# A new slot order for the delta stage, and smaller moves in the sparse, local and global stages of an eight-stage model on one Trainium2 core

## The chip, the cores and the metric

The kernel runs on one core of one Trainium2 chip. The time is the device time of one execution in microseconds (us). A kernel's time is the median of its runs; of the kernel before there are three, 3733.58, 3734.76 and 3739.41. Engines are named as in the profile: PE (TensorE's matmuls), PEld (its weight loads), DVE (VectorE), ACT (ScalarE), POOL (GpSimd) and SP (SyncE, which issues DMAs).

## The reference

A stream of rows of 128 features runs through eight layers, each a residual on the layer norm of what came before (X holds them in 16 tiles of 128 rows):

```
x = x + delta(ln(x))      # gated delta rule, 8 value heads of 128, then a mixture of 8 experts, top 2
x = x + ternary(ln(x))    # one linear layer with weights in -1, 0, 1
x = x + chunks(ln(x))     # attention in chunks of 32, and over their means
x = x + ternary(ln(x))
x = x + sparse(ln(x))     # 16 heads of 8; only the 10 top queries of a head attend
x = x + local(ln(x))      # two layers: windowed attention of 8 heads, then a gated MLP
x = x + grouped(ln(x))    # 16 query heads, 4 key heads of 64, rotary, full softmax
x = x + local(ln(x))      # again, same weights
```

The delta rule, for each token and each head, is

```
S = S * exp(g)
S = S + k (v - k S) * beta
o = q S
```

It is computed in 16 tiles of 128 tokens. Within a tile the chain of tokens becomes a triangular system, whose inverse Y is built in five doubling levels (blocks of 2 x 64 rows): turn Y, multiply it from the right with the system, multiply from the left, put the new blocks into Y. Between tiles only the state S is handed on.

In the sparse stage a head's output is softmax(q k) v, divided by the row's sum and set to nought where the query is not valid; the local stage first shifts tokens by one for half of the features; the global one takes an exact row maximum from "rough" scores ahead and subtracts it in the real ones.

## The kernel before

Each stage is one function, called by `build_program` in the order delta, ternary, chunks, ternary, sparse, local, global, local. Within a stage each engine has its own list of steps, all in one order written by hand; semaphores tie them. There is no planner: an engine does its list in order, and a step that must wait holds up all behind it.

**Delta** (`delta_block`). `SLOTS` runs over the tiles and some more; in slot n an engine does steps of several tiles: projections and qk norms of tile n or n-1, first levels of the triangular system of n-1, last levels and reads of the state of n-2, the state and core of n-3, the experts of n-4. PSUM is eight banks, given to the products by the constants in lines 347 to 349; a step waits until the bank's last reader is through. The steps of which the prediction speaks:

- PE: `project_q/k/v/v2/z` (L387, L391 to 424), `grams`, `turn_Y(n, l)` (L486) turns Y of level l, `right_products` (L538), `left_products` (L587), `read_by_keys` and `read_by_queries` (L601, L612) multiply with the state, `solved`, `intra`, `state_sums` (L631 and on), `turn_core` (L656).
- DVE: `residuals` (L1080, L1081), `decayed_reads` (L1085), `update_Y` (L1071), `beta_decays` (L1028), `system` (L1036), `first_Y` (L1056 a copy, L1057 a predicated copy), `decayed_updates`, `core_sums` (L1112 to L1115), `norms` (L3348 on, a helper of 9 small operations), `add_state` (L1104), which ends in `state_ready`.
- POOL: `gate_matrices` (L963), `masked_decays` (L970), `weigh_z` (L974), `scale_state` (L982).

The state's loop goes: `read_by_keys(n)` -> `residuals` -> `solved` -> `updates` -> `decayed_updates` -> `state_sums` -> `add_state` -> `read_by_keys(n + 1)`.

**Sparse** (`sparse_attention`). ACT makes exponentials of the 80 x 2048 scores of each of two halves (g = 0, 1) (L2139); `scale_probs` multiplies them by the row's weight on DVE (L2204); `turn_probs` turns them on PE (L2099); DVE copies them out (L2209); `contexts` is 16 tiles of 128 x 80 (L2106); `rows_out`, the copy to `ow` (L2144) and the product of rows y (L2125) follow.

**Local** (`local_layers`). 32 items (two layers over 16 tiles), slot after slot; `keep_tokens` (L2553, L2554) copies the turned rows from PSUM to hT for the projection (L2331); ACT's slot begins with the squares of q and k (L2505) and ends with `keep_probs` (L2561).

**Global** (`grouped_attention`). 32 units of 8 spans j; each has scores of its queries over the keys, in rough form for the maximum (`part_max`, L3257) and then for real (L2984, L2986), contexts (L2997) and sums. `project(("q", u + 2))` (L2953) makes the queries of two units ahead, `turn_max` (L2975) the row maxima, `place_max` (L3273) puts these into `global_mrow`, `swap_halves` (ACT), `rotate` and `join_rotated` (L3252) make the rotary form. Keys are projected for only some units (`next_keys`).

## Time and profile before

| | us |
|---|---|
| median of three runs | 3734.76 |
| profiled execution | 3737.75 |
| its span in the trace | 3736.0 |
| PE, DVE, ACT, POOL busy over the span | 3254.7, 2669.1, 1946.8, 1687.1 |
| delta | 0 to 1071 |
| ternary, chunks, ternary | 1071 to 1237.4 |
| sparse | 1237.4 to 1369.6 |
| local | 1369.6 to 1796.5 |
| global | 1796.5 to 3303.3 |
| local | 3303.3 to 3736 |

The stage borders are read from the first instruction of each stage in the timeline. A row of a timeline reads: start, duration, engine, line, operation, what it writes and reads, shape; what stands in brackets at its end is how long the engine was idle before it, and which instruction's end released it. PEclk is the clock granted to TensorE as a share of its full rate. Times are us unless marked ns.

### The profile page before, as it was taken

Reading aid. Unit: us, or ns where it says so; the run is one execution under the profiler, and the core shown is the slowest. Engines: PE = TensorE matmul, PEld = TensorE weight load, DVE = VectorE, ACT = ScalarE, POOL = GpSimd, SP = SyncE. Lnnn points to the kernel's source line nnn. Section 1 sums busy time; section 2 is a strip of 40 time slices with the busy share of each in tenths; the row PEclk is TensorE's granted clock in tenths of the full one; section 3 lists DMA queues with packets and bytes.
Section 4 is the critical chain, followed back from the end, with each engine's and each line's share of the span. In section 5 each row is a group of like instructions: output and inputs, shape, how many; then the busy total and the mean of one; then the engine's idle time right before and its main releaser. Section 6 shows DMA issues by size and latency. Waiting matters only on the chain. (4 is left out here: it accounts for less than half of the span.)

```text
span 3736.0 us, 70352 instructions
## 1 busy us (share of the span) xinstructions
PE 3254.7 (87%) x27870; PEld 1992.5 (53%) x27870; DVE 2669.1 (71%) x4726; ACT 1946.8 (52%) x3456; POOL 1687.1 (45%) x1133
## 2 busy tenths in 40 slices
PE   5999999999747368998699999999999999969997
PEld 3667777777636256777333333333333333337776
DVE  4667667676655857777677777787778777667776
ACT  2445444444423219999344444444444444439997
POOL 0121212121114226665166666666666666756664
PEclk8999999999968669999799999999999999979999
DMA  2000000000010010000100000000000000010000
GB/s 95 2 1 2 2 2 1 2 2 2 2 54 2 6 55 1 2 2 2 30 1 1 1 1 1 1 1 1 1 1 1 1 1 1 1 46 2 2 2 13
DMA packets 22482, 31.76 MB, mean 8 GB/s; under 512 B 8610, under 2 KB 18252, under 8 KB 20940
## 3 DMA queue, kind: packets, MB, share of 16 engines
q1 hardware_dynamic: 22156, 27.26, 2.2%
q8 instruction: 223, 3.65, 0.4%
q14 instruction: 103, 0.84, 0.1%
HBM read 26.20 MB, written 1.05 MB: 7 GB/s over the span
## 5 line engine op out<-in xcount | busy, mean ns | idle before, releaser
L3190 POOL TENSOR_TENSOR global_acc_pool<-global_acc_pool,global_probs 128x1024 f32<-128x1024 f32 x320 | 796.6, 2489 | 246.3 <-ACT global_probs L3131 222.3
L3131 ACT ACTIVATE global_probs<-global_ps 128x1024 f32<-128x1024 f32 x512 | 519.9, 1024 | 626.6 <-PE global_ps L2986 611.2
L3257 DVE TENSOR_REDUCE global_part<-global_ps 128x2 f32<-128x1024 f32 x512 | 622.7, 1218 | 304.3 <-PE global_ps L2968 304.1
L2986 PE MATMUL global_ps<-global_q,global_k 64*128 64x512 f32 x2048 | 529.8, 595 | 0.0
L2997 PE MATMUL global_ps<-global_probs,global_v 128*64 128x512 f32 x2048 | 495.7, 605 | 0.0
L970 POOL TENSOR_TENSOR delta_etm<-delta_et,C_tile 128x1024 f32<-128x1024 f32 x16 | 40.2, 2514 | 755.6 <-ACT delta_et L853 755.6
L2968 PE MATMUL global_ps<-global_khh,global_qhh 64*128 64x512 f32 x1024 | 307.1, 597 | 59.0 <-DVE global_part L3257 52.0
L2984 PE MATMUL global_ps<-global_mrow,global_first 64*128 64x512 f32 x1024 | 321.1, 624 | 0.0
L2968 PEld LDWEIGHTS global_ps<-global_khh,global_qhh 64*128 64x128 f32 x1024 | 97.2, 187 | 375.9 <-DVE global_part L3257 300.5
L2997 PEld LDWEIGHTS global_ps<-global_probs,global_v 128*64 128x64 f32 x2048 | 124.2, 136 | 266.0 <-issue 178.2
L1071 DVE COPY_PREDICATED delta_Yd<-delta_tri,delta_ps 64x512 f32<-64x512 uint32 x160 | 116.6, 729 | 191.3 <-PE delta_ps L587 188.8
L2986 PEld LDWEIGHTS global_ps<-global_q,global_k 64*128 64x128 f32 x2048 | 196.5, 188 | 91.6 <-issue 62.8
L387 PE MATMUL delta_ps<-delta_wconv,delta_x1T 128*128 128x512 f32 x512 | 236.4, 606 | 2.7 <-PEq L50 1.5
L2496 ACT ACTIVATE local_sm<-local_ps,local_nb,local_rn 128x128 f32<-128x128 f32 x512 | 226.3, 463 | 15.8 <-DVE local_nb L2682 14.5
L862 ACT ACTIVATE delta_NTp<-delta_ps 64x512 f32<-64x512 f32 x176 | 104.1, 591 | 242.6 <-PE delta_ps L538 219.6
L3190 DVE TENSOR_TENSOR global_acc<-global_acc,global_probs 128x1024 f32<-128x1024 f32 x128 | 215.2, 1681 | 7.9 <-ACT global_probs L3131 7.9
L3112 ACT ACTIVATE global_swapped<-global_ps 32x512 f32<-32x512 f32 x192 | 112.8, 588 | 144.2 <-PE global_ps L2953 142.3
L857 ACT ACTIVATE delta_T<-delta_ps 64x512 f32<-64x512 f32 x176 | 104.0, 591 | 132.0 <-PE delta_ps L486 128.7
L2984 PEld LDWEIGHTS global_ps<-global_mrow,global_first 64*128 64x128 f32 x1024 | 98.1, 188 | 111.7 <-issue 100.1
L2593 POOL TENSOR_TENSOR local_sm<-local_sm,local_rden 128x1024 f32<-128x1024 f32 x64 | 121.4, 1897 | 65.3 <-DVE local_rden L2725 65.1
L2638 POOL TENSOR_TENSOR local_qkr<-local_qkr,local_rn 128x512 f32<-128x512 f32 x64 | 70.5, 1102 | 174.6 <-DVE local_rn L3356 174.6
L387 PEld LDWEIGHTS delta_ps<-delta_wconv,delta_x1T 128*128 128x128 f32 x512 | 94.9, 193 | 101.3 <-issue 97.0
(584 smaller groups left out, 7090.5 us busy)
## 6 DMA issues: line engine op xcount, KB each, us to landing
delta_cw<-in_conv_taps SPq DMA_DIRECT2D x4, 1024.0 KB, 10.6
local_tab<-in_rot_tables SPq DMA_DIRECT2D x2, 2048.0 KB, 12.4
local_tab<-in_rot_tables SPq DMA_DIRECT2D x2, 1536.0 KB, 7.7
localw_wqkv<-in_L_ffn_wqkv SPq DMA_DIRECT2D x2, 768.0 KB
delta_wqkvz<-in_L_attn_a_W_qkvz SPq DMA_DIRECT2D x1, 1024.0 KB, 5.6
local_tab<-in_rot_tables SPq DMA_DIRECT2D x2, 512.0 KB, 4.2
global_cos<-in_rope_cos SPq DMA_DIRECT2D x8, 128.0 KB, 3.3
global_sin<-in_rope_sin SPq DMA_DIRECT2D x8, 128.0 KB, 3.3
```

The costliest lines, as they stand in the source:

```text
L387: mm = pe.matmul(banks(bank), x1T[:, P * n + j:P * n + j + P], wconv[:, j, column:column + 512], start=(j == 0), stop=(j == TAPS - 1))
L1071: ins = dve.copy_predicated(Yd[own, n % 2], over_middle(tri[own, l + 1], HV), blocks(DELTA_BANK + s)[own])
L2496: ins = act.activation(sm[:, k % 2, g, :], ps[:, SC + part, P * i:P * i + P], ACT.Exp, bias=nb[:, k % 2, g:g + 1], scale=rn[:, k % RN, hea ...
L2593: pool.tensor_tensor(sm[:, k % 2], sm[:, k % 2], over_inner(rden[:, k % 2, :], P), ALU.mult)\
L2968: mm = pe.matmul(ps[:, first_bank + s, :], qhh[own, u % 2, P * qt:P * qt + P], khh[own, group_of(u) % 2, BLK * c:BLK * c + BLK], start=Tru ...
L2984: pe.matmul(ps[:, 2 * (at % 2) + s, :], first[own, :], mrow[own, u % 2, :], start=True, stop=False)
L2986: mm = pe.matmul(ps[:, 2 * (at % 2) + s, :], k2[own, group_of(u) % 2, P * k:P * k + P], q[own, u % 3, :], start=False, stop=True)
L2997: mm = pe.matmul(ps[own, 4, :], v[:, k, HD * g:HD * g + HD], probs[:, at % RING, BLK * s:BLK * s + BLK], start=(k == 0), stop=(k == TILES ...
L3112: ins = act.activation(swapped[32 * a:32 * a + 32, :], ps[32 * b:32 * b + 32, proj_bank(n), :], ACT.Copy, scale=1.0 if a % 2 else -1.0)
L3131: act.activation(probs[:, at % RING, :], ps[:, 2 * (at % 2):2 * (at % 2) + 2, :].rearrange("p b n -> p (b n)"), ACT.Exp).then_inc(S["probs ...
L3190: ins = eng.tensor_tensor(sums[:, u % 2, :], sums[:, u % 2, :], probs[:, at % RING, :], ALU.add)
L3257: dve.tensor_reduce(part[:, u % 2, r % SLOTS, :], ps[:, rough_banks(r), :], X_AXIS, ALU.max)\
```

## The change

In the delta stage all engines get a new order within the slot, and the PSUM banks are given out anew; every wait that follows from these two is adapted. `SLOTS` has one more turn. Slot n now does q, k, v, v2 and decays of tile n, which were split between n and n + 1 before, and state_sums of n - 2, which was n - 3. In the sparse stage the weights of rows are applied in the copy to `ow`, and the contexts of both halves become one chain of 32 matmuls of 160 columns where there were two of 32 (16 tiles in two passes) with 80. In the local stage `keep_tokens` goes from ACT to DVE and is one slot earlier. In the global stage the projection of q stands behind the first contexts of span 0, not ahead of it, its rotation is one span later, and `place_max` stands ahead of the join of the keys.

The delta stage: constants, GpSimd's list and VectorE's list.

```diff
-QK_BANK, V_BANK, Z_BANK, QKT_BANK, DECAY_BANK, GRAM_BANK, KS_BANK, QS_BANK, W_BANK = 2, 2, 0, 2, 2, 2, 0, 4, 0
-INTRA_BANK, STATE_BANK, CORET_BANK, GATEUP_BANK, OUT_BANK, X2T_BANK, ROUTER_BANK, HIDT_BANK, DOWN_BANK = 0, 4, 6, 2, 3, 4, 4, 3, 5
-T_BANK, NTP_BANK, DELTA_BANK = 6, 4, 0
+QK_BANK, V_BANK, Z_BANK, QKT_BANK, DECAY_BANK, GRAM_BANK, KS_BANK, QS_BANK, W_BANK = 2, 2, 6, 0, 6, 2, 2, 0, 6
+INTRA_BANK, STATE_BANK, CORET_BANK, GATEUP_BANK, OUT_BANK, X2T_BANK, ROUTER_BANK, HIDT_BANK, DOWN_BANK = 0, 4, 4, 4, 3, 1, 2, 2, 5
+T_BANK, NTP_BANK, DELTA_BANK = 0, 4, 6
...
-SLOTS = range(0, TILES + 4)
+SLOTS = range(0, TILES + 5)
...
         for n in SLOTS:
-            if valid(n - 4):
-                weigh_z(n - 4)
+            if valid(n - 2):
+                scale_state(n - 2)
+            if valid(n):
+                gate_matrices(n)
             if valid(n - 1):
                 masked_decays(n - 1)
-            if valid(n):
-                gate_matrices(n)
-            if valid(n - 3):
-                scale_state(n - 3)
+            if valid(n - 2):
+                weigh_z(n - 2)
...
         for n in SLOTS:
-            if valid(n - 3):
-                decayed_updates(n - 3)
-                core_sums(n - 3)
             if 0 <= n - 1 < TILES + LAG_ROW:
                 norms(n - 1)
             if valid(n - 3):
                 add_state(n - 3)
-                normalize_core(n - 3)
+            if valid(n - 4):
+                normalize_rows_2(n - 4)
             if valid(n - 1):
                 scale_qk(n - 1)
-            if valid(n - 4):
-                normalize_rows_2(n - 4)
-            if valid(n - 2):
+            if valid(n - 3):
+                normalize_core(n - 3)
+            if valid(n - 2):
+                decayed_reads(n - 2)
                 residuals(n - 2)
-                decayed_reads(n - 2)
-            if valid(n - 1):
-                beta_decays(n - 1)
-            if valid(n - 2):
                 update_Y(n - 2, 2, 0)
                 update_Y(n - 2, 2, 1)
             if valid(n - 1):
-                probs(n - 1)
-            if valid(n - 4):
-                logits(n - 4)
-            if valid(n - 1):
+                beta_decays(n - 1)
                 system(n - 1)
                 first_Y(n - 1, 0)
                 first_Y(n - 1, 1)
-            if valid(n - 4):
-                choose(n - 4)
+                probs(n - 1)
             if valid(n - 2):
                 update_Y(n - 2, 3, 0)
                 update_Y(n - 2, 3, 1)
-            if valid(n - 3):
-                add_rows(n - 3)
             if valid(n - 4):
+                logits(n - 4)
+                choose(n - 4)
                 routes(n - 4)
+                hidden(n - 4)
             if valid(n - 1):
                 update_Y(n - 1, 0, 0)
                 update_Y(n - 1, 0, 1)
-            if valid(n - 4):
-                hidden(n - 4)
             if valid(n - 2):
                 update_Y(n - 2, 4, 0)
                 update_Y(n - 2, 4, 1)
+            if valid(n - 3):
+                add_rows(n - 3)
             if valid(n - 1):
                 update_Y(n - 1, 1, 0)
                 update_Y(n - 1, 1, 1)
             if valid(n - 2):
                 update_Y(n - 2, 5, 0)
+                updates(n - 2)
+                decayed_updates(n - 2)
+            if valid(n - 4):
+                add_experts(n - 4)
             if valid(n):
                 qk_sums(n)
             if valid(n - 2):
-                updates(n - 2)
-            if valid(n - 4):
-                add_experts(n - 4)
+                core_sums(n - 2)
```

PE's slot n after, tile in brackets, and ACT's changes:

```
PE:  read_by_queries(n-2) read_by_keys(n-2) turn_qk(n-1) left(n-2,2) turn_core(n-3) turn_x2(n-4)
     grams(n-1) turn_Y(n-2,3) project_z(n-1) right(n-2,3) turn_Y(n-1,0) left(n-2,3) right(n-1,0)
     router(n-4) turn_Y(n-2,4) gate_and_up(n-4) left(n-1,0) out_rows(n-3) right(n-2,4)
     turn_Y(n-1,1) left(n-2,4) right(n-1,1) turn_hidden(n-4) turn_Y(n-2,5) left(n-1,1)
     right(n-2,5) project_q(n) left(n-2,5) turn_Y(n-1,2) solved(n-2) down(n-4) project_k(n)
     intra(n-2) right(n-1,2) project_v(n) decays(n) state_sums(n-2) project_v2(n)
ACT: keep_hidT(n-5) first; place_blocks(n-3) early, not place_blocks(n-2) last; silu_qk(n-1) between
     keep_T and keep_NTp of (n-2,2); keep_qkT before keep_coreT; router_exp and silu_gate together
```

The sparse stage:

```diff
         def turn_probs(g):
-            pe.wait_ge(A["probs_ready"], g + 1)
+            pe.wait_ge(A["probs_exp"], g + 1)
...
-        def contexts(g):
-            pe.wait_ge(A["probsT_ready"], g + 1)
+        def contexts():
+            pe.wait_ge(A["probsT_ready"], 2)
             for t in range(TILES):
-                mm = pe.matmul(ps[:, 4 * g + 3, 0:HALF], v_all[:, t, :], probsT[:, g, t, :],
+                mm = pe.matmul(ps[:, 7, 0:H * TOP], v_all[:, t, :], probsT[:, :, t, :],
                                start=(t == 0), stop=(t == TILES - 1))
             mm.then_inc(A["o_ps"], 1)
 
         def rows_out(g):
-            pe.wait_ge(A["oT_ready"], g + 1)
+            pe.wait_ge(A["oT_ready"], 1)
             pe.matmul(ps[0:HALF, 5 + g, 0:DIM], oT[:, 8 * g:8 * g + 8, :].rearrange("p h r -> p (h r)"),
                       wT[:, 3, :], start=True, stop=True).then_inc(A["ow_ps"], 1)
 
         turn_probs(0)
-        contexts(0)
         turn_probs(1)
-        contexts(1)
+        contexts()
         rows_out(0)
         rows_out(1)
...
             act.wait_ge(A["ow_ps"], g + 1)
-            act.activation(ow[:, g, :], ps[0:HALF, 5 + g, 0:DIM], ACT.Copy).then_inc(A["ow_ready"], 1)
+            act.wait_ge(A["weights_ready"], g + 1)
+            act.activation(ow[:, g, :], ps[0:HALF, 5 + g, 0:DIM], ACT.Copy, scale=srow[:, g:g + 1]).then_inc(A["ow_ready"], 1)
...
-        def scale_probs(g):
+        def row_weights(g):
             dve.wait_ge(A["probs_exp"], g + 1)
             own = srow[:, g:g + 1]
             link(dve.reciprocal(own, own))
-            link(dve.tensor_tensor(own, own, valid[:], ALU.mult))
-            dve.tensor_scalar(probs[:, g, :], probs[:, g, :], own, None, ALU.mult).then_inc(A["probs_ready"], 1)
+            dve.tensor_tensor(own, own, valid[:], ALU.mult).then_inc(A["weights_ready"], 1)
...
-        def own_heads(g):
-            dve.wait_ge(A["o_ps"], g + 1)
-            own = slice(8 * g, 8 * g + 8)
-            dve.tensor_tensor(oT[:, own, :], heads(ps[:, 4 * g + 3, 0:HALF], 8), over_inner(hm[:, own], TOP), ALU.mult)\
-                .then_inc(A["oT_ready"], 1)
-
-        scale_probs(0)
-        scale_probs(1)
         keep_probs(0)
         keep_probs(1)
-        own_heads(0)
-        own_heads(1)
+        row_weights(0)
+        row_weights(1)
+        dve.wait_ge(A["o_ps"], 1)
+        dve.tensor_tensor(oT[:], heads(ps[:, 7, 0:H * TOP], H), over_inner(hm, TOP), ALU.mult)\
+            .then_inc(A["oT_ready"], 1)
```

The local stage, then the global stage (PE, ACT, DVE):

```diff
-SLOTS = range(-3, ITEMS + 7)
+SLOTS = range(-4, ITEMS + 7)
...
-        def keep_tokens(m):
-            t = m % TILES
-            act.wait_ge(S["xT_ps"], m + 1)
-            act.activation(hT[UP, tokens(t)], ps[UP, TURN, 0:P], ACT.Copy)
-            act.activation(hT[DOWN, P * t + 1:P * t + P + 1], ps[DOWN, TURN, 0:P], ACT.Copy)\
-                .then_inc(S["hT_ready"], 1)
-
...
                 gelu(n - 4)
-            if valid(n + 3):
-                keep_tokens(n + 3)
             if valid(n - 2):
                 keep_probs(n - 2)
...
+        def keep_tokens(m):
+            t = m % TILES
+            dve.wait_ge(S["xT_ps"], m + 1)
+            dve.tensor_copy(hT[UP, tokens(t)], ps[UP, TURN, 0:P])
+            dve.tensor_copy(hT[DOWN, P * t + 1:P * t + P + 1], ps[DOWN, TURN, 0:P])\
+                .then_inc(S["hT_ready"], 1)
...
                 row_stats(n - 2)
+            if valid(n + 4):
+                keep_tokens(n + 4)
...
         for u in range(UNITS):
             for j in range(SPANS):
-                if j == 0 and u + 2 < UNITS:
-                    pe.wait_ge(S["mrow_ready"], u + 1)
-                    project(pe, ("q", u + 2))
...
                 if j == 2 and u:
                     out_sums(pe, u - 1)
+                if j == 0 and u + 2 < UNITS:
+                    project(pe, ("q", u + 2))
                 if at + 1 + AHEAD < UNITS * SLOTS:
                     rough_scores(pe, at + 1 + AHEAD)
...
-                if j == 0 and u + 2 < UNITS:
+                if j == 1 and u + 2 < UNITS:
                     swap_halves(("q", u + 2))
...
-                if j == 0 and u + 2 < UNITS:
+                if j == 1 and u + 2 < UNITS:
                     rotate(("q", u + 2))
-                if j == 1 and u + 2 < UNITS:
+                if j == 2 and u + 2 < UNITS:
                     join_rotated(("q", u + 2))
...
                 if j == 6 and next_keys(u):
                     rotate(next_keys(u))
+                if j == 7 and u + 1 < UNITS:
+                    place_max(u + 1)
                 if j == 7 and next_keys(u):
                     join_rotated(next_keys(u))
-                if j == 7 and u + 1 < UNITS:
-                    place_max(u + 1)
```

## Rows read from the trace of the kernel before

**Rows 1.** The windows view by stages: us, busy (x) per engine, PEclk, DMA, GB/s

```profile
0.00:1071.00 1071.00, 942.14 (x11302) 711.65 (x11302) 686.77 (x1233) 447.11 (x621) 152.82 (x72) 0.96 0.03 10
...
1369.60:1796.50 426.90, 365.19 (x3836) 286.49 (x3836) 322.65 (x957) 370.56 (x955) 246.86 (x260) 0.96 0.04 14
```

**Rows 2.** Timeline of VectorE: state additions, the first and the last of 14

```profile
161.23 1.22 DVE L1104 TENSOR_TENSOR delta_state<-delta_ps,delta_state 128x1024 f32<-128x1024 f32 x1 [0.26 <-issue]
...
937.94 1.22 DVE L1104 TENSOR_TENSOR delta_state<-delta_ps,delta_state 128x1024 f32<-128x1024 f32 x1
```

**Rows 3.** Timeline of TensorE at the hole, and two windows behind it

```profile
460.39 1.33 PE L538 MATMUL delta_ps<-delta_T,delta_NT 64*64 64x64 f32 x32 [2.04 <-DVE delta_state L1104]
...
461.60:465.00 3.40, 3.40 (x12) 2.72 (x10) 2.44 (x4) 3.19 (x4) 0.00 (x0) 0.56 0.00 0
...
465.00:470.00 5.00, 5.00 (x60) 4.48 (x59) 4.72 (x4) 2.40 (x4) 0.00 (x0) 1.00 0.00 2
```

**Rows 4.** Timeline of VectorE and GpSimd ahead of a state addition

```profile
331.32 2.30 DVE L1113 TENSOR_TENSOR delta_sq<-delta_core 128x1024 f32<-128x1024 f32 x1
...
335.50 2.21 DVE L3348 TENSOR_SCALAR delta_rn<-delta_ss 128x17 int32<-128x17 int32 x1
...
332.50 2.88 POOL L982 TENSOR_TENSOR delta_state<-delta_state,delta_eg 128x1024 f32<-128x1024 f32 x1
```

**Rows 5.** One line each: min/median/max ns; and GpSimd's timeline at 945

```profile
L1028 DVE TENSOR_TENSOR delta_etb<-delta_et,delta_nbeta x16: 1214/1215/1787, 57.7 to 946.4; 128x1024 f32<-128x1024 f32 x16
...
945.12 1.99 POOL L982 TENSOR_TENSOR delta_state<-delta_state,delta_eg 128x1024 f32<-128x1024 f32 x1 [9.09 <-PE delta_ps L612]
...
L1056 DVE COPY delta_Yd<-C_tile x32: 418/422/426, 68.1 to 953.9; 64x512 f32<-64x512 f32 x32
...
L1057 DVE COPY_PREDICATED delta_Yd<-delta_tri,delta_NT x32: 726/740/753, 68.6 to 954.3; 64x512 f32<-64x512 uint32 x32
```

**Rows 6.** Timelines of the first local stage: three slot starts, TensorE's and VectorE's start

```profile
1427.62 1.05 ACT L2505 ACTIVATE local_qksq<-local_ps 128x1024 f32<-128x1024 f32 x1
...
1723.54 1.05 ACT L2505 ACTIVATE local_qksq<-local_ps 128x1024 f32<-128x1024 f32 x1
...
1734.92 1.05 ACT L2505 ACTIVATE local_qksq<-local_ps 128x1024 f32<-128x1024 f32 x1
...
1380.08 3.24 PE L2331 MATMUL local_ps<-localw_wqkv,local_hT 128*128 128x512 f32 x4
...
1382.16 0.22 DVE L2787 CAST local_identr<-C_tile 128x128 fp32r<-128x128 f32 x1
```

**Rows 7.** Timeline of the sparse stage, ScalarE then TensorE; one window at the query products

```profile
1329.23 0.19 ACT L2139 ACTIVATION_READ_ACCUMULATOR sparse_probs<-sparse_ps,sparse_mrow 80x1 f32 x1
...
1340.74 2.34 PE L2099 MATMUL sparse_ps<-C_tile,sparse_probs 80*128 80x80 f32 x16
...
1344.79 7.11 PE L2106 MATMUL sparse_ps<-sparse_probsT,sparse_v_all 128*128 128x80 f32 x32 [1.71 <-DVE sparse_probsT L2209]
...
1353.31 14.03 PE L2125 MATMUL sparse_ps<-sparse_ow,sparse_selT 80*128 80x128 f32 x64 [0.36 <-ACT sparse_ow L2144]
...
1309.70:1316.70 7.00, 7.00 (x34) 6.83 (x34) 4.64 (x22) 0.00 (x0) 0.00 (x0) 0.65 0.01 2
```

**Rows 8.** Timeline of the global stage: join, hole, turn_max starts, and one window

```profile
1990.07 1.71 DVE L3252 TENSOR_TENSOR global_k<-global_rot 128x512 f32<-128x512 f32 x1
...
1992.43 1.12 PE L2953 MATMUL global_ps<-global_xnT,globalw_wq 128*128 128x512 f32 x2 [1.70 <-DVE global_mrow L3273]
...
1995.00:1998.00 3.00, 3.00 (x12) 1.25 (x12) 0.13 (x1) 2.94 (x5) 0.26 (x1) 0.63 0.00 0
...
1985.11 0.33 PE L2975 MATMUL global_ps<-C_tile,global_nmx 128*128 128x128 f32 x1
...
2176.71 0.33 PE L2975 MATMUL global_ps<-C_tile,global_nmx 128*128 128x128 f32 x1
...
2220.03 0.33 PE L2975 MATMUL global_ps<-C_tile,global_nmx 128*128 128x128 f32 x1
```

More of the change, by code:

```diff
@@ L608, in read_by_queries @@
                     pe.wait_ge(S["qkT_ready"], n + 1)
-                    pe.wait_ge(PAIRED["NTp_ready"][n % 2], step(n, 2, 1))
+                    if n >= 1:
+                        pe.wait_ge(S["core_sums"], n)
+                    else:
+                        pe.wait_ge(PAIRED["T_ready"][n % 2], step(n, 2, 1))
                     for h in range(HK):
@@ L744, in _ @@
                 for n in SLOTS:
-                    if valid(n - 1):
-                        project_v(n - 1)
-                    if valid(n - 3):
-                        state_sums(n - 3)
-                    if valid(n - 1):
-                        project_v2(n - 1)
-                    if valid(n - 2):
-                        right_products(n - 2, 2)
-                        read_by_keys(n - 2)
-                    if valid(n - 3):
-                        turn_core(n - 3)
                     if valid(n - 2):
                         read_by_queries(n - 2)
+                        read_by_keys(n - 2)
                     if valid(n - 1):
@@ L761, in _ @@
                         left_products(n - 2, 2)
+                    if valid(n - 3):
+                        turn_core(n - 3)
                     if valid(n - 4):
@@ L818, in _ @@
                     if valid(n - 2):
-                        intra(n - 2)
+                        solved(n - 2)
+                    if valid(n - 4):
+                        down(n - 4)
+                    if valid(n):
+                        project_k(n)
+                    if valid(n - 2):
+                        intra(n - 2)
+                    if valid(n - 1):
+                        right_products(n - 1, 2)
+                    if valid(n):
+                        project_v(n)
+                        decays(n)
+                    if valid(n - 2):
+                        state_sums(n - 2)
+                    if valid(n):
+                        project_v2(n)
             @block.scalar
```

226 lines of the change are left out of this document (131 added, 95 removed).

## The prediction

> **What bounds the kernel now.** I read the stage windows first (one core, stages one after the other), then each stage's timeline. The delta stage is TensorE's: 942 of 1071 us busy at a granted clock of 0.96 [rows 1]. Its steady slot lasts (937.94 - 161.23)/13 = 59.75 us [rows 2], and the only large hole of TensorE in it is one of 2.0 us per slot behind VectorE's state addition (L1104) [rows 3]. The local stages are ScalarE's: 370.6 of 426.9 us [rows 1], 11.84 us per slot. The global stage is TensorE's, with a hole of 1.70 us in some of its units [rows 8]. The sparse stage is one chain over PE, DVE and ACT, in which every operation counts [rows 7].
>
> The sum is made against the profiled run, 3737.75 us, which is 3.0 above the median of 3734.76.
>
> **Delta: the hole that goes.** Ahead of the state addition VectorE does, before, decayed updates, core sums and norms. Two of these meet GpSimd: L1113 takes 2.30 us [rows 4], where L1028, of the same operands, takes 1.21 [rows 5], and L3348, only 17 columns wide, takes 2.21; exactly there GpSimd runs gate matrices, state scaling (L982, itself 2.88 where it takes 1.99 elsewhere) and z weights back to back [rows 4, 5]. After, core sums stand at the slot's end, GpSimd has nothing in flight there, and the chain is 9.1 - 1.1 - 2.0 = about 6 us. The state comes 11.5 us after project_k, by my count of L1112 to L1104 at free durations; PE gets to read_by_queries 13.5 us after it, since intra, right(2), v, decays, state_sums and v2 now stand between. So the hole closes: -2.0 us per slot. Behind it TensorE's granted clock was 0.56 for 3.4 us [rows 3], mostly the lower of its two levels (1.2 and 2.4 GHz), which costs 3.4 x 0.44 = 1.5 us; it does so in about every second slot (the starts of L1104 are 59.0 and 60.7 apart by turns), so another -0.8. That leaves 56.95.
>
> **Delta: the wait that comes.** GpSimd now starts at read_by_keys(n-2) (K) with scale_state, gate_matrices, masked_decays, weigh_z; K is also what VectorE's residuals wait for, and behind these stand, on VectorE, update_Y(2), beta_decays, system and both first_Y(n-1). TensorE waits for first_Y in turn_Y(n-1,0), having after K only left(2), turn_core, turn_x2, grams, turn_Y(3), z and right(3) to do, about 9.1 us. On VectorE the chain is 2 x 1.22 + 2 x 0.74 + 1.22 + 1.29 + 2 x (0.42 + 0.74) = 8.75, with links about 9.5 us: hole 0.4. But L1081, L1028 and the copy L1056 have only SBUF operands and meet GpSimd. The row for that is the last of L1028's 16, at 946.4, the only one that started behind a running L982 (945.12 to 947.11): 1.79 us, not 1.21 [rows 5]. L1056 and L1057 never met GpSimd before (418 to 426 and 726 to 753 ns) [rows 5], so their price has to be bounded: nothing, or all of the masked_decays (2.4 us) and gate (1.9 us) that lie there. With GpSimd and VectorE alternating I get L1081 +0.5, L1028 +0.8 and the copy +1.7, first_Y at K + 12.4, so a hole of about 3.35 us. That is 60.3 us per slot; behind so long a hole the clock probably falls again as behind the old one, I take two slots of three at 1.5: +1.0, 61.3. The other holes that I find (at turn_Y(n,1), left(n-1,4), right(n,1)) are 0.2 to 0.3 and replace ones of the same size. Moving projections one slot earlier and the new banks only change which wait is met first; I count them at nothing, the cover being the PE work ahead of each. 61.3 - 59.75 = +1.55, over 14 full slots: **+22 us**. Ends: 57.6 (copy not held up, hole 0.4 and 0.25 of others: -30) to 62.1 (low clock each time and the others: +33).
>
> The Trainium skill (SBUF — State Buffer, section "SBUF: two separate sides") has the same pair of ports behind both engines: an exclusive lock, kept for a whole instruction by whichever starts first. By that rule a VectorE operation that has started first makes GpSimd wait instead, and the chain would slip less than I count; the trace agrees as far as it goes, L982 having started first and L1028 having waited.
>
> **Local, twice.** ACT loses the two hT copies. The 25 slots from 1427.62 to 1723.54 take 11.84 each; the one behind them, 1723.54 to 1734.92, has no such copy and takes 11.38 [rows 6]. The difference, 0.46, less 0.02 for a row maximum that then comes last, times 25 is -10.9 per stage (bounds 0.35 to 0.57 per slot); VectorE, busy 323 of 427 us [rows 1], hides the copies at the slot's end. The start pays: hT of the first tile now comes only when DVE is through with the mask and identity casts, 1382.16 + 0.22, and two rounds of turn and copy behind that, so that project_qk (L2331) starts at about 1384.5, not at 1380.08 [rows 6]: +4.4. Net -6.5 per stage, **-13** for both (-20 to -9).
>
> **Sparse.** Scaling leaves the chain; the weights go into the ow copy on ACT, which has slack since they are ready long before the contexts. turn_probs(1) can start when the second exponential ends, 1329.42; from its start to the contexts it was 1344.79 - 1340.74 = 4.05, so the joined contexts start at 1333.5 [rows 7]. The query products (L2079), 32 matmuls of 160 columns, took 7.0 us at a granted clock of 0.65 [rows 7]; at the lower level that is 9.1, at the upper 4.5. They end at 1342.6, where the old ones ended at 1351.9; the rows y (L2125) keep their distance of 1.4: start 1344.1 instead of 1353.31. **-9** (matmuls of 7 us: -11; of 4.5: -14; one us of order lost: -8).
>
> **Global.** In units that join keys, DVE's join (1.71) stands ahead of place_max, and TensorE waits 1.70 us in project(q) for it, then runs at a granted clock of 0.63 [rows 8]. A plain unit lasts 43.32, as from 2176.71 to 2220.03 (turn_max, L2975, one of 14 such). The stretch 1985.11 to 2176.71 is four units: 191.6 [rows 8]. The two others of this kind took 190.1 and 191.8; sum 573.5. After: place_max stands ahead of the join and the projection behind the first contexts, so the row maxima come 1.71 us earlier, which is all of the hole of 1.70: they are ready as TensorE gets to the scores. Four units are 4 x 43.32, three key projections of 1.25 and 0.3 for each late join: 178.3. That is 573.5 - 535 = **-39**, and -1 for units that are not in a stretch. If only the hole goes and the clock does not rise, 12 x 1.7 = 20; if the join then holds up part_max by its 1.71 and nothing hides it, -20 as well. Bounds -24 to -55 (holes of 0.4 in plain units gone too). Moving q's rotation from j 0 to 1 costs at most the 0.3 per unit that lies under TensorE's work.
>
> **Sum.** 3737.75 + 22 - 13 - 9 - 40 = 3697.75; less 3.0 for the median: **3695**.
>
> **The rivals.** (A) The copy wins: first_Y is not held up, the slot is 57.6, delta -30. For it: the same copies never took over 0.43 us. Against it: they never met GpSimd. 3695 - 52 = 3643. Chance 0.27. (B) The change does not do in the global stage what it says: the maxima are late all the same, since rough scores and part_max of the span before set them, and the hole moves to the scores; -10 and not -40: 3725. For it: 1.71 and 1.70 leave nothing to spare. Chance 0.12. (C) Slower: the new hole of 3.4 us in the delta stage is followed by the low clock not for 3.4 us of work but for all up to the next full slot. It decides at a slot of 64.8 us, that is 5.05 x 14 = +70, eating the -62 of the others and 7.5 beyond; this takes 6.5 us more of TensorE's work at half speed than I count. Against it: behind the hole at 460.39 the clock was 1.00 again from 465 on [rows 3]. At 65 us it gives 3695 - 22 + 74 = 3747. Chance 0.05. The forecast itself: 0.56.
>
> **How the numbers follow.** 3695 is the forecast's. Its own range is 3672 (sparse -14, local -20, global -51) to 3717 (delta +33; sparse, local and global half way to their small ends, +1, +2 and +8). The 8-in-10 range goes from below A (global gain 10 more than counted) to B: 3632 to 3724. About 0.2%, 7.5 us, is what a measurement of this kernel can tell from no change; 3727 is its lower edge. Faster: forecast 0.56, A 0.27, 0.05 of B's: 0.88. Same: the rest of B's, 0.07. Slower: 0.05.
>
> **What would show it.** In the profile after: no hole in front of L601 and L1113 at 1.22 (right), a wait of TensorE in turn_Y (L486) for first_Y (L1057) of 3 us and a copy L1056 near 2 us (right; at 0.42 it is A); slots of L1104 at 61.3; 11.40 between L2505 starts; L2975 starts 43 to 45 apart all along; L2125 9 us earlier after its stage begins. Wrong would be a gap in front of a step that I took for covered: state_sums or decays waiting for UD, or qk's silu one slot late.

## The result and the profile after

The changed kernel takes 3646.05 us in the median of four runs (3643.54 to 3650.88), beside 3736.91 for the kernel before (four runs). The ratio is 0.9759, with a 95% interval of 0.9744 to 0.9773: 91 us or 2.4% faster. The forecast was 3695, its range 3632 to 3724. The profiled execution took 3643.54 us, its span is 3641.8.

Stage by stage, each counted from its first instruction to that of the next (the last one to the end of the span; some 4 us ahead of the delta stage are not counted), the two profiled spans differ so:

| stage | before, us | after, us | difference | forecast |
|---|---|---|---|---|
| delta | 1071.2 | 1074.8 | +3.6 | +22 |
| ternary, chunks, ternary | 162.1 | 160.6 | -1.5 | 0 |
| sparse | 132.2 | 114.3 | -17.9 | -9 |
| local, first | 427.0 | 421.4 | -5.6 | -6.5 |
| global | 1508.2 | 1438.5 | -69.7 | -40 |
| local, second | 431.2 | 428.3 | -2.9 | -6.5 |

The windows view of after, one row per stage that was changed (columns as in [rows 1]):

```profile
0.00:1074.80 1074.80, 940.45 (x11302) 720.19 (x11302) 689.10 (x1234) 444.78 (x621) 169.73 (x72) 0.94 0.03 10
...
1239.30:1353.60 114.30, 53.16 (x296) 41.85 (x296) 79.68 (x176) 26.50 (x38) 32.57 (x18) 0.70 0.00 1
1353.60:1775.00 421.40, 368.43 (x3836) 285.21 (x3836) 338.63 (x1021) 353.31 (x891) 246.94 (x261) 0.95 0.04 14
1775.00:3213.50 1438.50, 1381.89 (x6704) 565.21 (x6704) 1120.38 (x1099) 686.63 (x798) 956.88 (x421) 0.99 0.01 3
3213.50:3641.80 428.30, 369.15 (x3836) 286.33 (x3836) 338.15 (x1021) 353.19 (x891) 247.22 (x260) 0.95 0.04 14
```

Beside [rows 1] the reader sees the ScalarE time of a local stage fall from 370.6 to 353.3 us, and VectorE's rise from 322.7 to 338.6. In the delta stage TensorE is busy for as long as before (940 and 942 us), yet at a clock of 0.94, where it was 0.96.

**The delta slot.** Windows over the same 13 slots, from the first to the 14th state addition (L1104, now L1150, and L1153 in the third), of before, of after, and of an experiment told below (e3_pool_reads):

```profile
161.23:937.94 776.71, 732.48 (x9119) 555.73 (x9120) 527.95 (x892) 351.20 (x488) 122.29 (x51) 0.98 0.01 2
```

```profile
153.32:941.63 788.31, 733.35 (x9121) 564.45 (x9120) 534.13 (x893) 349.17 (x489) 136.75 (x52) 0.97 0.01 2
```

```profile
148.86:881.51 732.65, 718.39 (x9121) 549.35 (x9120) 502.95 (x893) 349.19 (x489) 109.55 (x52) 1.00 0.01 2
```

The slot is 776.7/13 = 59.75 us before and 788.3/13 = 60.64 after. TensorE's work is the same; at a granted clock of 1.00 throughout, as in the third row, it takes 718.4/13 = 55.3 us. So before was 55.3 + 1.1 of low clock + 3.4 idle, and after is 55.3 + 1.1 + 4.2. This is the forecast's picture: the hole in front of the state reads is gone, and there is one of 3.2 us in front of turn_Y(n-1,0) (L500), and a lower clock behind it. TensorE's, then VectorE's timeline of after, then GpSimd's, in the slot from 455 to 517:

```profile
474.47 1.98 PE L500 MATMUL delta_ps<-C_tile,delta_Yd 64*64 64x64 f32 x32 [3.21 <-DVE delta_Yd L1103]
...
463.25 1.76 DVE L1127 TENSOR_TENSOR delta_R<-delta_val,delta_R 128x1024 f32<-128x1024 f32 x1
...
466.47 1.38 DVE L1074 TENSOR_TENSOR delta_etb<-delta_et,delta_nbeta 128x1024 f32<-128x1024 f32 x1
...
469.26 1.09 DVE L1102 COPY delta_Yd<-C_tile 64x512 f32<-64x512 f32 x1
470.39 2.76 DVE L1103 COPY_PREDICATED delta_Yd<-delta_tri,delta_NT 64x512 f32<-64x512 uint32 x1
473.18 0.42 DVE L1102 COPY delta_Yd<-C_tile 64x512 f32<-64x512 f32 x1
...
463.89 2.88 POOL L1009 TENSOR_TENSOR delta_gm<-C_tile,delta_g 128x1024 f32<-128x1024 f32 x1
466.73 3.34 POOL L1016 TENSOR_TENSOR delta_etm<-delta_et,C_tile 128x1024 f32<-128x1024 f32 x1
470.03 2.54 POOL L1020 TENSOR_TENSOR delta_zs<-delta_zs,delta_gnw 128x1024 f32<-128x1024 f32 x1
```

The copy L1102 takes 1.09 us and not 0.42, the predicated copy L1103 2.76 and not 0.73; both start while GpSimd's masked decays (L1016) and z weights (L1020) run. Only the first of the two pairs is hit, the second (473.18) is at its old length. It is so in nearly every slot.

### The profile page after: what moved, and what is told of

It is laid out like the page before. It is cut to its first block and busy times, and to the rows that moved or that the text cites. A ratio compares the mean times of both kernels' runs of the same rounds, so it can differ in the third digit from the quotient of the medians.

```text
span 3641.8 us, 70299 instructions
## 1 busy us (share of the span) xinstructions
PE 3215.8 (88%) x27838; PEld 1983.2 (54%) x27838; DVE 2666.1 (73%) x4851; ACT 1909.5 (52%) x3328; POOL 1711.3 (47%) x1133
## 5 line engine op out<-in xcount | busy, mean ns | idle before, releaser
L3164 ACT ACTIVATE global_probs<-global_ps 128x1024 f32<-128x1024 f32 x512 | 519.1, 1024 | 511.0 <-PE global_ps L3020 497.6
L1028 POOL TENSOR_TENSOR delta_state<-delta_state,delta_eg 128x1024 f32<-128x1024 f32 x16 | 30.4, 1897 | 784.6 <-PE delta_ps L636 784.6
L3002 PE MATMUL global_ps<-global_khh,global_qhh 64*128 64x512 f32 x1024 | 314.4, 611 | 26.8 <-DVE global_part L3290 19.1
L3223 DVE TENSOR_TENSOR global_acc<-global_acc,global_probs 128x1024 f32<-128x1024 f32 x128 | 189.5, 1480 | 7.9 <-ACT global_probs L3164 7.9
L500 PE MATMUL delta_ps<-C_tile,delta_Yd 64*64 64x64 f32 x2816 | 118.0, 231 | 59.5 <-DVE delta_Yd L1103 48.7
```

Of the source, the lines that this page charges most:

```text
L500: mm = pe.matmul(blocks(T_BANK + s)[BLOCK[s], h, :], Yd[BLOCK[s], n % 2, h, :], ident[BLOCK[s], BLOCK[s]], start=True, stop=True)
L3002: mm = pe.matmul(ps[:, first_bank + s, :], qhh[own, u % 2, P * qt:P * qt + P], khh[own, group_of(u) % 2, BLK * c:BLK * c + BLK], start=Tru ...
L3164: act.activation(probs[:, at % RING, :], ps[:, 2 * (at % 2):2 * (at % 2) + 2, :].rearrange("p b n -> p (b n)"), ACT.Exp).then_inc(S["probs ...
L3223: ins = eng.tensor_tensor(sums[:, u % 2, :], sums[:, u % 2, :], probs[:, at % RING, :], ALU.add)
```

## The experiments

Kernels timed in several rounds are given with their interval; for the others the stages are read from the trace, where a stage that was left alone differs by up to 6 us from one execution to the next (the delta stage of before: 1065.3 to 1071.2; the global one: 1503.5 to 1508.2, and only the profiled execution of before has the 1508.2).

**Each stage's part alone.** Four kernels, each the kernel before with one of the four functions (`delta_block`, `sparse_attention`, `local_layers`, `grouped_attention`) taken from after.

> The new delta stage alone, the other stages as before. Theory: the stages do not touch each other, so this gives what the two traces show for the stage, 1074.8 where it ended at 1071.4: +3 us, with a hole of 3.2 us in each slot in front of turn_Y(n-1,0). Rival (forecast): +22 us, if the lag at the start and the end of the whole kernel hid the cost of the slots; then the slot is 61.3 and not 60.6. Rival A: -30, the copy is not held up.

> The new sparse stage alone. Theory: -18 us as in the trace of after (112.7 where it was 130.7), 6.6 of it in the rows y, which run at the higher clock. Rival: the clock in y came from the timing of the stages ahead and not from the stage's own edits; then -11 or so, y (L2125 before) at 14 us as before.

> The new local stage alone, in both its places. Theory: -0.35 us per slot at 25 to 30 slots, twice, less 4.6 twice for the start: -8 to -13. Rival: nothing, since what ACT gives up is taken by another wait in the slot (then the slot stays above 11.7).

> The new global stage alone. Theory: -70 us, of which the three stretches with keys give 43 (3 x 14.5) and the plain units 1.04 each. Forecast: -40, plain units stay at 43.3. The plain unit tells them apart: 42.3 or 43.3.

| kernel | ratio (95%) | us | stage in the trace |
|---|---|---|---|
| e1_delta | 1.0011 (1.0000 to 1.0022) | +4 | 1073.5 |
| e1_sparse | 0.9964 (0.9952 to 0.9976) | -13 | 114.2 |
| e1_local | 0.9985 (0.9974 to 0.9997) | -6 | first 420.9; second 418.6 to its last instruction (423.0 before) |
| e1_global | 0.9813 (0.9794 to 0.9831) | -70 | 1439.5 |

The sum is -85, against -91 for all four together: the stages add up within the intervals (that of e1_global alone is 7 us to either side), and no effect of one part on another is seen. The new delta stage alone costs neither the forecast's +22 nor gives rival A's -30. In e1_sparse the rows y take 7.41 us, so their clock comes from the stage's own edits. The local slot is 11.5, not above 11.7. The plain unit of the global stage is 42.3.

**Who makes the new hole of the delta stage.** e2_pool is the kernel after with GpSimd's slot in another order:

```diff
                 for n in SLOTS:
+                    if valid(n - 1):
+                        masked_decays(n - 1)
+                        pool.wait_ge(PAIRED["Y_ready"][(n - 1) % 2], Y_step(n - 1, 0, 1))
                     if valid(n - 2):
                         scale_state(n - 2)
                     if valid(n):
                         gate_matrices(n)
-                    if valid(n - 1):
-                        masked_decays(n - 1)
                     if valid(n - 2):
                         weigh_z(n - 2)
```

> The kernel after, with one thing changed in the delta stage: GpSimd does masked_decays first, then waits until both first_Y are done, and only then scales the state, makes gate matrices and weighs z. Theory (GpSimd's operations hold up L1127, L1074, L1102 and L1103 on VectorE, and these make TensorE's hole of 3.2 us): those four run at 1.22, 1.21, 0.42 and 0.74, the hole goes to about 0.4, the slot from 60.6 to some 55.5 (3.2 less 0.4, and 2.5 of low clock behind it): -60 to -75 us, near 3580. Rival (the wait is only VectorE's own chain of 9.5 us): the hole stays above 2.5 us and the time within 10 us of that after the change; GpSimd being late would then even cost.

Measured: 3602.34 us, ratio 0.9646 (0.9630 to 0.9662), some 44 us under after; the delta stage is 1028.5 us, its steady slot 57.79 (60.9 in after, where the mean of 60.64 has a shorter first slot in it). The four operations of VectorE are at their free length in every slot but the edge ones (the copy: 419 to 425 ns in all 32), and no wait of TensorE for first_Y is left. So the cause is settled: GpSimd's operations made the hole, not VectorE's own chain. The size fell short by 16 to 31 us; the moved operation meets VectorE at a new place, and a hole of 1.11 us per slot appears there, 14 us over the 13 slots. GpSimd's, VectorE's and TensorE's timeline of e2_pool:

```profile
433.55 2.34 POOL L1016 TENSOR_TENSOR delta_etm<-delta_et,C_tile 128x1024 f32<-128x1024 f32 x1 [34.22 <-ACT delta_et L904]
...
433.62 2.30 DVE L3390 SCALAR_TENSOR_TENSOR delta_rn<-delta_rtmp,delta_rn 128x17 f32<-128x17 f32 x1
...
499.92 0.30 PE L429 MATMUL delta_ps<-C_tile,delta_qn 128*128 128x128 f32 x1 [1.11 <-DVE delta_qs L1132]
```

L3390 works on 17 columns. It starts 0.07 us behind GpSimd and ends with it. e3_pool_reads adds a wait to e2_pool, which puts the masked decays beside operations that read PSUM:

```diff
                     if valid(n - 1):
+                        if valid(n - 2):
+                            pool.wait_ge(S["qS_ps"], n - 1)
                         masked_decays(n - 1)
```

> As e2_pool, but masked_decays also waits for read_by_queries(n-2), so that it runs beside L1132 and L1127, which read PSUM. In e2_pool it started at 433.55, the last operation of the norms (L3390, 17 columns) at 433.62 and took 2.30 us, and TensorE had a hole of 1.11 us in front of turn_qk. Theory (an operation of VectorE with only SBUF operands that starts behind a GpSimd one waits for its end, one with a PSUM operand does not): L3390 back at 0.18, L1132 and L1127 at 1.22 under it, the hole of 1.11 gone, slot 57.79 -> 56.7, -15 us against e2_pool: near 3587. Rival (GpSimd slows every VectorE operation beside it): L1132 or L1127 take over 2 us, the residuals come 1 to 2 us later, and the time stays within 5 us of e2_pool or rises.

Measured: 3583.83 us, ratio 0.9591 (0.9575 to 0.9607), 18.5 below e2_pool in the medians. The steady slot is 56.57. GpSimd's timeline, then VectorE's:

```profile
490.32 2.37 POOL L1016 TENSOR_TENSOR delta_etm<-delta_et,C_tile 128x1024 f32<-128x1024 f32 x1 [39.78 <-PE delta_ps L650]
...
490.28 1.22 DVE L1134 TENSOR_TENSOR delta_qs<-delta_ps,delta_eg 128x1024 f32<-128x1024 f32 x1
492.01 1.23 DVE L1129 TENSOR_TENSOR delta_R<-delta_ps,delta_eg 128x1024 f32<-128x1024 f32 x1 [0.50 <-PE delta_ps L636]
...
498.58 0.42 DVE L1105 COPY delta_Yd<-C_tile 64x512 f32<-64x512 f32 x1
499.03 0.72 DVE L1106 COPY_PREDICATED delta_Yd<-delta_tri,delta_NT 64x512 f32<-64x512 uint32 x1
```

L1134 and L1129, which read PSUM, run under L1016 at their own 1.22 us; the rival, that GpSimd slows whatever stands beside it, is out. TensorE is at a clock of 1.00 over all 13 slots and idle for 1.1 us in each (third window above).

The Trainium skill (SBUF — State Buffer, section "SBUF: two separate sides") has an exclusive lock on one pair of ports, between a GpSimd operation and a VectorE one with two SBUF inputs or in a two-port mode, for the whole length of whichever starts first. These traces agree: 2.30 us where 0.18 is usual, behind L1016, nothing for the two with a PSUM input, and on the other side GpSimd's gate matrices at 2.88 us instead of 1.90 behind L1127.

**The sparse stage's clock.** y ran at 7.41 us in place of 14.03 [rows 7], which the forecast did not have. e2_contexts is after with the contexts in two chains again (VectorE's step behind them goes half by half again as well, which is left out here):

```diff
-                def contexts():
-                    pe.wait_ge(A["probsT_ready"], 2)
+                def contexts(g):
+                    pe.wait_ge(A["probsT_ready"], g + 1)
                     for t in range(TILES):
-                        mm = pe.matmul(ps[:, 7, 0:H * TOP], v_all[:, t, :], probsT[:, :, t, :],
+                        mm = pe.matmul(ps[:, 4 * g + 3, 0:HALF], v_all[:, t, :], probsT[:, g, t, :],
...
                 turn_probs(0)
+                contexts(0)
                 turn_probs(1)
-                contexts()
+                contexts(1)
```

> The kernel after, with the sparse contexts in two chains of 80 columns again, one behind each half's copy; weights stay in the copy to ow. Theory (the clock rose within the 160-column contexts and stayed): the clock stays at 0.50 through contexts and y, y takes 14.0 us again, the stage 112.7 + 6.6 + about 5 = 124. Rival (the clock rose because the chain has shorter pauses): y stays at 7.4 us and the stage is near 117.

e4_scale is after with one chain, but the probabilities scaled on VectorE ahead of the turns, as before:

```diff
-                    pe.wait_ge(A["probs_exp"], g + 1)
+                    pe.wait_ge(A["weights_ready"], g + 1)
...
-                    dve.tensor_tensor(own, own, valid[:], ALU.mult).then_inc(A["weights_ready"], 1)
+                    link(dve.tensor_tensor(own, own, valid[:], ALU.mult))
+                    dve.tensor_scalar(probs[:, g, :], probs[:, g, :], own, None, ALU.mult).then_inc(A["weights_ready"], 1)
...
+                row_weights(0)
+                row_weights(1)
                 keep_probs(0)
                 keep_probs(1)
-                row_weights(0)
-                row_weights(1)
...
-                    act.activation(ow[:, g, :], ps[0:HALF, 5 + g, 0:DIM], ACT.Copy, scale=srow[:, g:g + 1])
+                    act.activation(ow[:, g, :], ps[0:HALF, 5 + g, 0:DIM], ACT.Copy)
```

> The kernel after with the sparse probabilities scaled on VectorE again ahead of the turns (two operations, 2.04 and 1.28 us before), contexts still in one chain of 160 columns. Theory (the columns of the contexts alone decide the clock of the rows y): y stays at 7.4 us and the stage is 112.7 + 2 = 115, since the second turn comes some 2 us later. Rival (the shorter pause ahead of the turns matters to the clock as well): contexts at 0.50 throughout and y at 14.0 us, the stage near 122.

TensorE's timeline, windows of the contexts and one of y, in after, in e2_contexts, and in e4_scale:

```profile
1335.45 6.87 PE L2146 MATMUL sparse_ps<-sparse_probsT,sparse_v_all 128*128 128x160 f32 x32 [1.71 <-DVE sparse_probsT L2248]
...
1343.90 7.41 PE L2164 MATMUL sparse_ps<-sparse_ow,sparse_selT 80*128 80x128 f32 x64 [0.49 <-ACT sparse_ow L2184]
...
1335.45:1339.00 3.55, 3.55 (x13) 3.55 (x14) 0.40 (x4) 0.00 (x0) 0.00 (x0) 0.50 0.00 0
...
1339.00:1342.30 3.30, 3.30 (x21) 3.08 (x19) 0.00 (x0) 0.00 (x0) 0.00 (x0) 0.83 0.00 0
...
1346.00:1351.30 5.30, 5.30 (x48) 5.12 (x46) 2.08 (x3) 0.00 (x0) 0.00 (x0) 1.00 0.00 0
```

```profile
1341.18 7.12 PE L2146 MATMUL sparse_ps<-sparse_probsT,sparse_v_all 128*128 128x80 f32 x32 [1.71 <-DVE sparse_probsT L2249]
...
1349.80 14.02 PE L2165 MATMUL sparse_ps<-sparse_ow,sparse_selT 80*128 80x128 f32 x64 [0.45 <-ACT sparse_ow L2185]
...
1341.20:1345.00 3.80, 3.80 (x18) 3.80 (x19) 0.54 (x4) 0.00 (x0) 0.00 (x0) 0.50 0.00 0
...
1351.00:1363.00 12.00, 12.00 (x59) 12.00 (x58) 2.07 (x3) 0.00 (x0) 0.00 (x0) 0.50 0.00 0
```

```profile
1336.98 7.44 PE L2146 MATMUL sparse_ps<-sparse_probsT,sparse_v_all 128*128 128x160 f32 x32 [1.71 <-DVE sparse_probsT L2248]
...
1345.87 7.41 PE L2164 MATMUL sparse_ps<-sparse_ow,sparse_selT 80*128 80x128 f32 x64 [0.36 <-ACT sparse_ow L2183]
...
1346.00:1353.00 7.00, 7.00 (x63) 7.00 (x64) 2.07 (x3) 0.00 (x0) 0.00 (x0) 1.00 0.00 0
```

With 80 columns the clock stays at 0.50 from the contexts to the end of y, and the stage is 125.9 us from its first to its last instruction (112.7 in after, 130.7 before). With 160 columns it rises within the contexts, whether the scaling is there or not (115.5 us). So the rise goes with the joined chain, and not with the scaling or the longer pause that it makes ahead of the turns. Joining changes two things at once, the columns of a matmul (160 for 80) and the order of the steps (both turns stand ahead of it), and no run takes these apart. Joining is worth 13 us, of which 6.6 lie in y, and leaving out the scaling is worth 2.8.

**The global stage.** e2_place is the kernel before with one edit, e2_rotate with another (the queries' swap, rotation and join one span later, the projection where it was), e4_place_rotate with both:

```diff
+                        if j == 7 and u + 1 < UNITS:
+                            place_max(u + 1)
                         if j == 7 and next_keys(u):
                             join_rotated(next_keys(u))
-                        if j == 7 and u + 1 < UNITS:
-                            place_max(u + 1)
```

```diff
-                        if j == 0 and u + 2 < UNITS:
+                        if j == 1 and u + 2 < UNITS:
                             swap_halves(("q", u + 2))
...
-                        if j == 0 and u + 2 < UNITS:
+                        if j == 1 and u + 2 < UNITS:
                             rotate(("q", u + 2))
-                        if j == 1 and u + 2 < UNITS:
+                        if j == 2 and u + 2 < UNITS:
                             join_rotated(("q", u + 2))
```

> The kernel before with place_max ahead of the join of keys, and nothing else. Theory: the hole of 1.70 us and the low clock behind it go, the three stretches with keys fall from 191 to about 178 us, plain units stay at 43.3; global stage -36 to -40. Rival: the projection's place is needed as well, the stretches stay above 185.

> The kernel before with swap, rotation and join of the queries one span later, TensorE's projection where it was, and nothing else. Theory (the three holes of 0.3 to 0.45 us of a plain unit come from part_max behind the rotation and the join): plain units 43.3 -> 42.3, stretches with keys keep their holes; global stage -25 to -33. Rival (the projection's new place is what shortens the unit): 43.3 stays.

> The kernel before with both e2_place's and e2_rotate's edit in the global stage; TensorE's projection of the queries stays ahead of the scores. Each alone gave a stage of 1475.9 and 1481.1 us where it is 1503.5 to 1508.2 before and 1438.5 to 1440.2 with all three edits. Theory (the two add up and the projection's place gives the rest): near 1449, plain unit 42.5, four units with keys near 178. Rival (the two overlap, since both take load off VectorE at the same place, and the projection's place is worth over 20 us): above 1455.

Starts of turn_max in the timeline (the first two enclose four units with keys, the last two a plain one), of e2_place, e2_rotate and after:

```profile
1978.33 0.33 PE L2975 MATMUL global_ps<-C_tile,global_nmx 128*128 128x128 f32 x1
...
2159.99 0.33 PE L2975 MATMUL global_ps<-C_tile,global_nmx 128*128 128x128 f32 x1
...
2203.31 0.33 PE L2975 MATMUL global_ps<-C_tile,global_nmx 128*128 128x128 f32 x1
```

```profile
1978.85 0.33 PE L2975 MATMUL global_ps<-C_tile,global_nmx 128*128 128x128 f32 x1
...
2166.11 0.33 PE L2975 MATMUL global_ps<-C_tile,global_nmx 128*128 128x128 f32 x1
...
2208.60 0.33 PE L2975 MATMUL global_ps<-C_tile,global_nmx 128*128 128x128 f32 x1
```

```profile
1955.74 0.33 PE L3009 MATMUL global_ps<-C_tile,global_nmx 128*128 128x128 f32 x1
...
2131.55 0.33 PE L3009 MATMUL global_ps<-C_tile,global_nmx 128*128 128x128 f32 x1
...
2173.83 0.33 PE L3009 MATMUL global_ps<-C_tile,global_nmx 128*128 128x128 f32 x1
```

| | four units with keys | plain unit | stage |
|---|---|---|---|
| before [rows 8] | 191.6 | 43.32 | 1508.2 |
| e2_place | 181.7 | 43.32 | 1475.9 |
| e2_rotate | 187.3 | 42.49 | 1481.1 |
| e4_place_rotate | 175.8 | 42.48 | 1447.3 |
| after | 175.8 | 42.28 | 1438.5 |

place_max alone gives -32, a little less than its theory: each of the four units is 1.2 us longer than a plain one plus its share of the key projections (45.4 on the mean, where 43.3 and three projections in four make 44.3), and I had counted 0.3 for the join that is now behind place_max. The later rotation alone gives -27, as its theory has it, though its plain unit is 42.49 and not 42.3. Both together give -61, where -59 was expected. All of these are counted from the 1508.2 of the profiled execution; from the other three executions of that stage (1503.5 to 1504.0) they are -28, -23 and -57, so that the sum is met to within 6 us rather than 2. The projection's place is worth the last 7 to 9 us (1438.5 to 1440.2 in all traces with the three edits). Its rival of over 20 us falls.

**The local stage's start.** e3_start is e3_pool_reads with one more edit:

```diff
-                for first in range(GROUP, TILES, GROUP):
-                    normalize_group(first)
+                dve.wait_ge(S["filled"], 1)
+                for m, first in enumerate(range(GROUP, TILES, GROUP)):
+                    keep_tokens(m)
+                    normalize_group(first)
...
-                dve.wait_ge(S["filled"], 1)
...
-                    if valid(n + 4):
+                    if valid(n + 4) and n + 4 >= TILES // GROUP - 1:
                         keep_tokens(n + 4)
```

> As e3_pool_reads, and in both local stages the first three keep_tokens stand between the groups of the normalization, with the casts of mask and identity behind them. Theory (the 4.4 to 4.9 us lost at the start of each local stage come from the place of those copies alone): project_qk starts about 3.8 us earlier in the stage, -7.6 us against e3_pool_reads. Rival: the start is then set by the wait for weights or by rotate behind the casts, and under half of it comes back.

Timelines of after, whose local stage begins at 1353.6, and of e3_start, where it begins at 1292.2 (first copy of hT, first projection):

```profile
1366.30 0.27 DVE L2787 COPY local_hT<-local_ps 64x128 f32<-64x128 f32 x1
...
1368.49 3.62 PE L2365 MATMUL local_ps<-localw_wqkv,local_hT 128*128 128x512 f32 x4
```

```profile
1301.02 0.28 DVE L2790 COPY local_hT<-local_ps 64x128 f32<-64x128 f32 x1
...
1303.78 2.77 PE L2368 MATMUL local_ps<-localw_wqkv,local_hT 128*128 128x512 f32 x3
```

The projection starts 11.6 us into the stage; in after it is 14.9, and before it was 10.5 ([rows 6], from 1369.6). That is 3.3 per stage, where the theory had 3.8. Measured: 3574.35 us, ratio 0.9568 (0.9552 to 0.9584), 9.5 below e3_pool_reads. In the two traces the first local stage is 5.4 us shorter and the second 0.8: behind its last slot start the second lasts 56.6 us, not 54.8, and the granted clock from there to the last result was 0.87, not 0.93. It is the fastest kernel of the study, 72 us under after and 160 under before.

## Why the prediction was wrong

The direction was right, and in each part what was forecast to go did go; the size was not, 40 us where it is 91. The step that failed most is the price of moving q's rotation, put at a cost of at most 0.3 us per unit, where the move gave 0.8 back in each of 30 units; behind it come the clock of the sparse rows y and the ends of the delta stage, both put at nothing. Step by step:

**Delta, the hole that goes:** right. No wait of TensorE for the state is left, L1113 (now L1159) takes 1.22 us in all 16 slots, and the norms run free.

**Delta, the wait that comes:** right in place, cause and nearly in size: 3.35 us counted, 3.2 measured; 1.0 us per slot for the low clock counted, 1.1 measured (the old slot had 1.1 of it too, where I took 0.8). I had L1028 held up for 0.8 us and the copy L1056 for 1.7; the trace has 0.2 and 0.7 on these and 2.0 on the predicated copy behind them. The slot came out at 60.64 and not 61.3, as the other holes, which I kept at 1.4 us, are 1.0, and TensorE's own work is 55.3 where the sum has 55.55.

**Delta, the sum:** wrong. I took 14 slots times the difference and nothing for the ends. The 13 slots gave +11.6 where 22 was counted; the first state addition comes at 153.32 and not at 161.23 [rows 2], which is -7.9, so that the stage is at +3.6. The 161.23 is the latest of seven executions of the old stage (157.7 to 161.2, against 153.0 to 153.3 for the new one), so the start gives 4 to 8 us. What makes them was not tested. By the windows above TensorE is idle for 5.4 us less and busy for 2.6 us less outside the 13 slots; the term "Moving projections one slot earlier ... I count them at nothing" is where I would look.

**Sparse:** -18 in place of -9. The term that was mis-sized is "They end at 1342.6 ... the rows y keep their distance": I let the low clock last through the contexts, 9.1 us, and let y keep its 14. The 32 matmuls of 160 columns took 6.87 us, of which the last part ran at the full clock, and y 7.41. These are the 2.2 and 6.6 us that were missing; that the contexts would start where they did was right.

**Local:** -5.6 and -2.9 in the spans, -6 together in e1_local (-1 to -10), where I had -13. The start cost what I had worked out: 14.9 us to the projection and not 10.5. The slot gave less; ScalarE's timeline of after, three starts of a slot:

```profile
1418.03 1.05 ACT L2539 ACTIVATE local_qksq<-local_ps 128x1024 f32<-128x1024 f32 x1
...
1429.53 1.05 ACT L2539 ACTIVATE local_qksq<-local_ps 128x1024 f32<-128x1024 f32 x1
...
1441.05 1.04 ACT L2539 ACTIVATE local_qksq<-local_ps 128x1024 f32<-128x1024 f32 x1
```

11.51 in the first layer, 11.47 in the second, against 11.84 before and 11.40 counted. The term that was mis-sized is "The difference, 0.46, less 0.02": it is 0.33 to 0.37 per slot. Over the same 25 slots the two stages gave -8.4 and -9.0, not -10.9 each; what holds the slot above the 11.38 of one without a copy was not found. The second stage ends 2.1 us later behind its last slot start, and TensorE's clock was lower there:

```profile
3683.20:3727.40 44.20, 32.72 (x354) 28.68 (x352) 26.84 (x102) 28.49 (x72) 16.00 (x22) 0.96 0.01 1
```

```profile
3586.90:3633.10 46.20, 34.43 (x354) 30.13 (x352) 26.89 (x102) 28.66 (x72) 15.99 (x21) 0.93 0.01 2
```

The first window is of before, the second of after; the same 354 matmuls took 1.7 us longer.

**Global:** -70 (-63 to -70 over the executions) in place of -40, the largest miss. The step that failed is "Moving q's rotation from j 0 to 1 costs at most the 0.3 per unit". I priced this edit as a cost only and put the holes of a plain unit into the bound. Most of them were the rotation's. VectorE's timeline of before has it in a plain unit:

```profile
2189.17 2.25 DVE L3190 TENSOR_TENSOR global_acc<-global_acc,global_probs 128x1024 f32<-128x1024 f32 x1
...
2192.48 1.93 DVE L3252 TENSOR_TENSOR global_q<-global_rot 128x512 f32<-128x512 f32 x1
```

An addition held up to 2.25 us (1.22 is usual) and a join of 1.93 follow one another there, a part_max waits behind each, and TensorE behind these (holes of 0.42 and 0.30 us at 2192.61 and 2195.60). With the rotation a span later the join is held up too, even to 2.33 us, but no held-up addition stands just ahead of it. TensorE's waits for part_max in one plain unit (total, times, longest), of before and of e2_rotate:

```profile
PE global_ps L2968 <- DVE global_part L3257: 1.2, 3, 0.5
```

```profile
PE global_ps L2968 <- DVE global_part L3257: 0.6, 1, 0.6
```

Every unit that rotates queries pays, 30 of 32; moved, it gives 0.83 in a plain unit, and 30 times that is 25 us, where the stage gave 23 to 27. It does not depend on the keys: the four units with keys gave 4.3. For place_max I had -39 and it gave -32 (-28 by the other executions), and the projection's place, for which I had no term of its own, gave 7 to 9.

**The rivals.** The measured time is that of rival A, 3643, and by this alone A would look confirmed. It is not: A says that the copy is not held up and the delta stage gains 30 us, and both are false. That the total fits is luck: sparse and global gained 39 us more than I had, and the delta stage cost 18 us less. Rival B, no gain for the global hole, and C, a low clock over most of a slot, were both wrong.

## What to carry to other kernels

- Of an operation that is moved on a loaded engine, look up what stands directly behind it at the old place, and who waits for that: here a rotation that could as well come a span later cost 0.8 us in each of 30 units.
- Where GpSimd and VectorE share a slot, start GpSimd's long operations beside VectorE's reads of PSUM. Another order and two waits on GpSimd gave 62 us here (3646 to 3584), where the new order of all engines had left its stage 4 us longer.
- A total that fits confirms no mechanism. Read each stage's difference first.

## What the runs showed of the hardware that was not expected

- A 17-column operation that starts 0.07 us behind a GpSimd operation of 1024 columns takes 2.30 us; two VectorE operations of 1024 columns with a PSUM input, beside the same one, take 1.22 each.
- The granted clock rose from 0.50 to 1.00 in a chain of 32 matmuls of 160 columns and then stayed up over 64 matmuls of 128 columns (7.41 us). Behind a chain of as many matmuls of 80 columns it stayed at 0.50, and the same 64 took 14.02. TensorE was busy all through either chain.
- At a clock of 0.50 a matmul of 160 columns came every 0.27 us and one of 80 every 0.21 (13 in the first 3.55 us of the one chain, 18 in 3.80 of the other), so twice the columns took a quarter longer. Two chains of 80 columns took 14.2 us together, the joined one of 160 columns 6.87 to 7.44, a part of it at 1.00.
